# An idle row copied ahead of ScalarE's last chunk, and eight tokens' adds given to GpSimd

## The chip, the cores and the metric

One core of a Trainium2 chip runs the whole program. The metric is the time of one execution on the device in microseconds (us): lower is better. Three runs of the kernel before gave 105.50, 105.60 and 105.89 us, median 105.60 us.

## What is computed

The input `x` is (2, 2048, 512), and `cond` is (2, 512). A rate neuron turns each channel into spikes, and a two-layer network is applied to the spikes, with w1 (512, 2048) and w2 (2048, 512):

```python
rates = relu(x) * 0.001
c = cond[:, None, :] + cumsum(rates, axis=1)
fl = floor(c)
prev = concatenate([floor(cond)[:, None, :], fl[:, :-1, :]], axis=1)
spikes = (fl - prev) / 0.001
h = relu(spikes @ w1 + b1)
out = x + h @ w2 + b2
```

A channel's sum rises so slowly that it crosses a whole number about once in 2048 tokens. So nearly every token has no spike at all, and its output is `x` plus one fixed row, `relu(b1) @ w2 + b2`. This is called the idle row. The tokens with a spike are the exceptions.

## The kernel before

**Layout.** Each batch of 2048 tokens lies in SBUF as `x_sb[b]`, 128 partitions by 16 tokens by 512 channels, in float32. Four tokens of the 16 make a piece (`TQ = 4`), and a piece is the unit in which the result goes out: 1 MB, eight pieces in all. "Piece (b, q)" is tokens 4q to 4q+3 of batch b.

**Loading.** SyncE loads the x blocks and the sixteen row pairs of w1 transposed and w2. While they arrive, ScalarE makes from each chunk m of w1 the change that one spike of each channel makes in the hidden layer (`table_chunk`), TensorE multiplies it by w2 into the four PSUM banks `ps_table` (`table_part(m, begin, end)`: the column blocks begin to end of chunk m), and VectorE sums x by blocks of 16 tokens.

**The idle row.** VectorE sums five of the sixteen terms in `idle_part`. TensorE adds the others in strips of 32 partitions (`add_strips`) in `ps_idle`. ScalarE copies the strips to `idle_base`, TensorE joins them into the full row on all partitions (`join_strips`, again in `ps_idle`), and ScalarE copies that to SBUF as `idle_row`. VectorE can read the row from PSUM, and GpSimd reads the SBUF copy. Both have a function `add_idle(b, begin, end)`, which adds the row to the tokens begin to end of batch b. VectorE's is one instruction for the whole stretch, and GpSimd's is one instruction for each token.

**VectorE's chain.** For each batch, VectorE finds which token each channel spikes in (`find_tokens`), TensorE spreads these over all partitions (`spread_tokens`), VectorE compares them (`count_met`, four instructions `same`) and marks the first channel of each token (`find_leads`), TensorE counts (`count_leads`), VectorE makes a one-hot table (`find_slots`, outputs `slot` and `hot`), TensorE turns this into a list (`list_rows`), and VectorE writes row numbers (`list_rows`, output `row_at`). GpSimd then gathers rows of w1 by these numbers (`get_rows(b)`, two indirect DMAs to `spiking_rows`). After batch 1's list come `find_row_tokens`, TensorE's `spread_row_tokens` and VectorE's `turn_others`. From there on TensorE runs the two layers for the tokens in which several channels spike (`first_layer`, `second_layer`). Small operations for checks and lists follow on VectorE: `find_odd`, `count_crowd`, `list_singles`, `list_general`, `judge`.

**Output.** SyncE issues one 1 MB store per piece, in a fixed order, and waits before each for the piece's `idle_added`. Once all four stores of a batch have landed (`idle_stored[b]`), GpSimd issues four indirect DMAs (L368, `add_row`) that add table rows to the tokens with a single spike. Between the two batches' adds it gathers a row of x (L403). At the end it writes the several-spike tokens' rows (L414), which need TensorE's second layer and the `row_ready` that VectorE raises.

**What sets the order.** Each engine runs its own instructions in the order written, and the engines wait for each other on semaphores only. The semaphore `reading_psum` is raised by VectorE at the start of `count_met(1)` and again after `find_row_tokens`. GpSimd waits for it before its adds.

## Time and profile before

| | us |
|---|---|
| median of three runs | 105.60 |
| the profiled execution, whole | 105.66 |
| its span, first to last instruction | 103.9 |
| TensorE (PE) busy | 89.3 (86%) |
| VectorE (DVE) busy | 72.3 (70%) |
| GpSimd (POOL) busy | 45.5 (44%) |
| ScalarE (ACT) busy | 35.6 (34%) |

1.76 us of the execution lie outside the span. The mean granted TensorE clock is 0.95 of full speed. The program loads for the first 45 us or so, computes lists while the DMA engines are nearly idle, and from about 66 us on writes its output.

### The profile page before, as it was taken

What the parts mean: (1) busy time and instruction counts of PE and PEld (TensorE: products, weight loads), DVE (VectorE), ACT (ScalarE), POOL (GpSimd) and SP (SyncE); (2) the same over time, 40 slices, a digit from 0 to 9 for tenths busy, and PEclk for the clock granted to TensorE, in tenths of its full rate; (3) what the DMA queues carried; (4) which work ended last, traced back from release to release, by engine and by line L of the source; (5) the groups of instructions that cost most, each with busy time, mean ns of one, the idle gap of its engine ahead of it and who ended that gap; (6) DMA issues with size and microseconds to landing.
All of it is one profiled execution on the core that took longest, in us unless ns stands there. A gap on an engine that the chain in (4) does not pass through costs nothing.

```text
span 103.9 us, 1032 instructions
## 1 busy us (share of the span) xinstructions
PE 89.3 (86%) x299; PEld 44.9 (43%) x299; DVE 72.3 (70%) x164; ACT 35.6 (34%) x64; POOL 45.5 (44%) x46
## 2 busy tenths in 40 slices
PE   5999999998999999899999999992999999990000
PEld 5944444442644423552345444422997445420000
DVE  2439899999695969899896998699999912002200
ACT  2867525325255550579071000061677000000000
POOL 6598000000077600037303802899900478747860
PEclk9999999999999999999999999999589999999655
DMA  2999999999999999930000610599999999997881
GB/s 77 298 378 393 413 423 413 412 408 402 413 412 408 390 398 392 406 151 8 6 3 0 145 70 0 180 363 372 410 432 404 416 416 321 297 208 144 100 115 62
DMA packets 8491, 28.72 MB, mean 276 GB/s; under 512 B 2024, under 2 KB 2152, under 8 KB 7303
## 3 DMA queue, kind: packets, MB, share of 16 engines
q1 hardware_dynamic: 6192, 25.43, 62.8%
q0 software_dynamic: 2144, 3.17, 15.1%
q8 instruction: 4, 0.07, 0.3%
q14 instruction: 5, 0.04, 0.1%
q10 hardware_dynamic: 146, 0.01, 0.1%
HBM read 21.58 MB, written 10.75 MB: 311 GB/s over the span
## 4 chain that ended last, share of the span: by engine, by line
SPq 21%; PE 19%; DVE 17%; DMA 16%; POOL 11%; issue 10%; POOLq 3%; DVEq 0%
DMA x_sb<-in_x 16%; PE ps_table L868 13%; SPq L290 13%; POOL out L368 9%; SPq L285 7%; DVE x_sb L737 7%; DVE over_two L710 4%; DVE same L645 3%; POOLq L60 2%; PE ps_idle L884 2%; DVE total_two L592 1%; PE ps_turn L905 1%; POOL out L414 1%; POOL general_x L403 1%; PE ps_idle L894 1%
## 5 line engine op out<-in xcount | busy, mean ns | idle before, releaser
L868 PE MATMUL ps_table<-w_sb 128*128 128x512 f32 x128 | 57.8, 598 | 0.0
L868 PEld LDWEIGHTS ps_table<-w_sb 128*128 128x128 f32 x128 | 23.2, 190 | 27.4 <-issue 25.1
L363 POOL DMA_INDIRECT rates<-in_x_turned,sixteen_at x8 | 9.3, 1166 | 31.4 <-DVE sixteen_at L606 29.6
L592 DVE SCALAR_TENSOR_TENSOR total_two<-x_sb,total_two 128x1024 f32<-128x1024 f32 x14 | 17.1, 1224 | 2.4 <-DMA x_sb<-in_x 2.1
L457 ACT ACTIVATE w_sb<-w_sb,b_col 128x512 f32<-128x512 f32 (+2 forms) x19 | 12.2, 643 | 16.9 <-DMA w_sb<-in_w_pairs 16.9
L368 POOL DMA_INDIRECT out<-w_sb,to_single x8 | 12.4, 1555 | 10.4 <-issue 8.6
L737 DVE TENSOR_TENSOR x_sb<-x_sb,ps_idle 128x2048 f32<-128x2048 f32 (+2 forms) x8 | 13.8, 1750 | 0.7 <-DVE row_token L694 0.2
L974 PE MATMUL ps_met<-w_sb 128*128 128x512 f32 x32 | 14.2, 596 | 0.0
L458 ACT ACTIVATE w_sb<-w_sb,minus_relu_b 128x512 f32<-128x512 f32 (+2 forms) x19 | 12.3, 649 | 0.6
L375 POOL TENSOR_TENSOR x_sb<-x_sb,idle_row 128x512 f32<-128x512 f32 x8 | 9.9, 1265 | 0.1
L974 PEld LDWEIGHTS ps_met<-w_sb 128*128 128x128 f32 x32 | 5.9, 190 | 6.7 <-issue 6.5
L387 POOL DMA_INDIRECT spiking_rows<-in_w,row_at x4 | 4.0, 1006 | 10.6 <-DVE row_at L680 9.9
L493 ACT ACTIVATE w_sb<-ps_table 128x512 f32<-128x512 f32 x4 | 2.4, 597 | 13.3 <-PE ps_table L868 13.3
L788 DVE TENSOR_TENSOR general_x<-general_x,b_row 128x512 f32<-128x512 f32 x1 | 0.7, 693 | 8.0 <-DMA general_x<-in_x,from_general 8.0
L548 DVE SCALAR_TENSOR_TENSOR idle_part<-w_sb,relu_b,idle_part 128x512 f32<-128x512 f32 x5 | 3.8, 758 | 2.0 <-DMA w_sb<-in_w_pairs 1.9
L979 PE MATMUL ps_small<-ones 128*128 128x128 f32 x16 | 3.7, 429 | 1.1 <-POOLq L337 1.1
L979 PEld LDWEIGHTS ps_small<-ones 128*128 128x128 f32 x16 | 3.5, 331 | 1.1 <-POOLq L337 1.1
L955 PE MATMUL ps_turn<-ident,spiking_rows 128*128 128x128 f32 x6 | 2.0, 328 | 2.2 <-issue 2.2
L710 DVE TENSOR_TENSOR over_two<-block_sum,theta_sum 128x8 f32<-128x8 f32 x1 | 3.7, 3726 | 0.0
L354 POOL MEMSET spiking_rows<- 128x2048 f32 x2 | 3.5, 1798 | 0.0
L645 DVE SCALAR_TENSOR_TENSOR same<-ps_turn,token,weigh 128x512 bf16<-128x512 f32 x4 | 3.0, 751 | 0.7 <-PE ps_turn L917 0.6
L884 PE MATMUL ps_idle<-w_sb,relu_b 128*32 128x512 f32 x22 | 3.2, 604 | 0.0
(142 smaller groups left out, 84.8 us busy)
## 6 DMA issues: line engine op xcount, KB each, us to landing
x_sb<-in_x SPq DMA_DIRECT2D x16, 512.0 KB, 14.7
out<-x_sb SPq DMA_DIRECT2D x8, 1024.0 KB, 7.9
w_sb<-in_w_pairs SPq DMA_DIRECT2D x15, 512.0 KB, 16.0
w_sb<-in_w_pairs SPq DMA_DIRECT2D x2, 256.0 KB, 2.9
b_row<-in_b SPq DMA_DIRECT2D x1, 256.0 KB, 14.7
rates<-in_x_turned,sixteen_at POOLq DMA_INDIRECT x8, 6.2
out<-w_sb,to_single POOLq DMA_INDIRECT x8, 6.3
spiking_rows<-in_w,row_at POOLq DMA_INDIRECT x4, 4.2
```

The costliest lines, as they stand in the source:

```text
L285: sp.dma_start(w_sb[:, m, :, :], w_pairs[m * P:(m + 1) * P, :, :]).then_inc(w_in[m], 16)
L290: sp.dma_start(x_sb[b][:, tokens, :], x_blk[b, :, tokens, :]).then_inc(x_in[b][half], 16)
L363: pool.indirect_dma_start(out=rates[:, col, :], out_offset=None, in_=x_sixteen, in_offset=bass.IndirectOffsetOnAxis(ap=sixteen_at[:, col:c ...
L368: pool.indirect_dma_start(out=out_rows, out_offset=bass.IndirectOffsetOnAxis(ap=to, axis=0), in_=row, in_offset=None, bounds_check=last_ro ...
L375: last = pool.tensor_tensor(x_sb[b][:, t, :], x_sb[b][:, t, :], idle_row[:, :], ALU.add)
L457: chain(act.activation(weights, weights, ACT.Relu, bias=b1_col[:, m:m + 1], scale=PER_DT))
L458: act.activation(weights, weights, ACT.Identity, bias=minus_relu_b1[:, m:m + 1]).then_inc(table_hidden_ready, 1)
L592: chain(dve.scalar_tensor_tensor(out=total_two[b][:, :, :], in0=tokens, scalar=0.0, in1=total_two[b][:, :, :], op0=ALU.max, op1=ALU.add))
L710: dve.tensor_tensor(over_two[:, :].rearrange("p (b c) -> p b c", b=B), block_sum[:, :, :, P], theta_sum[:, 1, :].rearrange("p (b c) -> p b ...
L737: last = dve.tensor_tensor(tokens, tokens, along(ps_idle[:, :], end - begin), ALU.add)
L868: last = pe.matmul(ps_table[c][:, :], table_hidden[:, m, c * P:(c + 1) * P], w2_sb[:, m, :], start=(m == 0), stop=(m == FC - 1))
L974: last = pe.matmul(to[:, :], hidden[m], w2_sb[:, m, :], start=(m == 0), stop=(m == FC - 1))
```

## The change

Four things change.

1. In TensorE's order, all strips are added together, and the join follows one column block later, ahead of `count_leads(0)`.
2. ScalarE copies the joined row to `idle_row` ahead of chunk 15's two activations instead of behind them.
3. GpSimd adds the row to tokens 0 and 1 of batch 0 as soon as the copy is there, then issues `get_rows(0)`, adds to tokens 2 to 5, issues `get_rows(1)` and adds to tokens 6 and 7. None of these eight adds waits for `reading_psum`. Tokens 12 to 15 of batch 1 stay with GpSimd and wait for `reading_psum` 2. GpSimd has twelve adds instead of eight.
4. VectorE loses its adds for tokens 0 to 7 of batch 0 and gets tokens 12 to 15 of it. All its adds stand behind `turn_others`, and the small operations stand ahead of it. SyncE stores in the order (0,0), (0,1), (0,2), (0,3), (1,0), (1,1), (1,3), (1,2).

```diff
@@ SyncE
-            for b, q in ((0, 0), (0, 3), (0, 1), (0, 2), (1, 3), (1, 0), (1, 1), (1, 2)):
+            for b, q in ((0, 0), (0, 1), (0, 2), (0, 3), (1, 0), (1, 1), (1, 3), (1, 2)):
@@ GpSimd
+            pool.wait_ge(idle_copied, 1)
+            add_idle(0, 0, 2)
             get_rows(0)
-            pool.wait_ge(idle_copied, 1)
-            pool.wait_ge(reading_psum, 1)
-            add_idle(0, 12, 13)
+            add_idle(0, 2, 6)
             get_rows(1)
+            add_idle(0, 6, 8)
             pool.wait_ge(reading_psum, 2)
-            add_idle(0, 13, 16)
             add_idle(1, 12, 16)
@@ ScalarE
                 if m == FC - 2:
                     act.wait_ge(strips_summed, 1)
                     act.activation(idle_base[:, :], ps_idle[:, :], ACT.Copy).then_inc(strips_copied, 1)
-            act.wait_ge(idle_summed, 1)
-            act.activation(idle_row[:, :], ps_idle[:, :], ACT.Copy).then_inc(idle_copied, 1)
+                    act.wait_ge(idle_summed, 1)
+                    act.activation(idle_row[:, :], ps_idle[:, :], ACT.Copy).then_inc(idle_copied, 1)
@@ VectorE
             find_leads(1)
-            add_idle(0, 0, 1)
             find_slots(1)
-            add_idle(0, 1, 2)
             list_rows(1)
             find_row_tokens()
-            dve.sem_inc(reading_psum, 1)
-            add_idle(0, 2, 4)
-            turn_others()
-            add_idle(0, 4, 8)
-            add_idle(0, 8, 12)
             find_odd()
             count_crowd()
-            add_idle(1, 0, 4)
             list_singles()
             list_general()
+            turn_others()
+            dve.sem_inc(reading_psum, 1)
+            add_idle(0, 8, 12)
+            add_idle(0, 12, 16)
+            add_idle(1, 0, 4)
             add_idle(1, 4, 8)
             add_idle(1, 8, 12)
             judge()
@@ TensorE
-            add_strips(4, 8)
-            table_part(11, 0, 2)
+            add_strips(4, FC - BY_HAND + 1)
+            table_part(11, 0, 1)
+            join_strips()
             count_leads(0)
-            table_part(11, 2, 3)
-            add_strips(8, FC - BY_HAND + 1)
-            table_part(11, 3, DC)
-            join_strips()
+            table_part(11, 1, DC)
             list_rows(0)
```

GpSimd's instructions from the last gather of x (L363) to the first scatter-add (L368), before:

```order
L363 DMA rates<-in_x_turned,sixteen_at 128x16 [waits sixteen_listed]
L363 DMA rates<-in_x_turned,sixteen_at 128x16 x3
L387 DMA spiking_rows<-in_w,row_at 128x2048 [waits rows_listed,rows_cleared]
L387 DMA spiking_rows<-in_w,row_at 128x2048 [waits rows_listed]
L375 TENSOR_TENSOR x_sb<-x_sb,idle_row 128x512 [waits reading_psum,idle_copied]
L387 DMA spiking_rows<-in_w,row_at 128x2048 [waits rows_got0,rows_listed,rows_cleared]
L387 DMA spiking_rows<-in_w,row_at 128x2048 [waits rows_got1,rows_listed]
L375 TENSOR_TENSOR x_sb<-x_sb,idle_row 128x512 [waits reading_psum]
L375 TENSOR_TENSOR x_sb<-x_sb,idle_row 128x512 x6
L368 DMA out<-w_sb,to_single 4096x512 [waits table_rows_ready,idle_stored0,singles_listed]
```

The same place on GpSimd in the changed kernel:

```order
L375 TENSOR_TENSOR x_sb<-x_sb,idle_row 128x512 [waits idle_copied]
L375 TENSOR_TENSOR x_sb<-x_sb,idle_row 128x512
L387 DMA spiking_rows<-in_w,row_at 128x2048 [waits rows_listed,rows_cleared]
L387 DMA spiking_rows<-in_w,row_at 128x2048 [waits rows_listed]
L375 TENSOR_TENSOR x_sb<-x_sb,idle_row 128x512 x4
L387 DMA spiking_rows<-in_w,row_at 128x2048 [waits rows_got0,rows_listed,rows_cleared]
L387 DMA spiking_rows<-in_w,row_at 128x2048 [waits rows_got1,rows_listed]
L375 TENSOR_TENSOR x_sb<-x_sb,idle_row 128x512 x2
L375 TENSOR_TENSOR x_sb<-x_sb,idle_row 128x512 [waits reading_psum]
L375 TENSOR_TENSOR x_sb<-x_sb,idle_row 128x512 x3
```

Two adds now stand ahead of the first pair of gathers, and four ahead of the second pair, where there was one.

TensorE around the join of the strips (`ps_idle<-idle_base,strip_first`) and batch 0's count (`leads_run,upper`), before:

```order
L884 MATMUL ps_idle<-w_sb,relu_b 32x512 x4
L868 MATMUL ps_table<-w_sb 128x512 x2
L923 MATMUL ps_small<-leads_run,upper 128x2
L868 MATMUL ps_table<-w_sb 128x512
L884 MATMUL ps_idle<-w_sb,relu_b 32x512 x3
L888 MATMUL ps_idle<-idle_part,ones 32x512
L868 MATMUL ps_table<-w_sb 128x512
L894 MATMUL ps_idle<-idle_base,strip_first 128x512
L938 MATMUL ps_small<-named,hot 128x4 x4
```

The same place on TensorE in the changed kernel, whose lines are numbered three lower:

```order
L881 MATMUL ps_idle<-w_sb,relu_b 32x512 x7
L885 MATMUL ps_idle<-idle_part,ones 32x512
L865 MATMUL ps_table<-w_sb 128x512
L891 MATMUL ps_idle<-idle_base,strip_first 128x512
L920 MATMUL ps_small<-leads_run,upper 128x2
L865 MATMUL ps_table<-w_sb 128x512 x3
L935 MATMUL ps_small<-named,hot 128x4 x4
```

The join moved ahead of the count and of three of chunk 11's column blocks. What TensorE does up to `list_rows(0)` is the same in sum.

## Rows read from the trace of the kernel before

**Rows 1.** Timeline of GpSimd, last part: start, length, line, operation, [idle before <-releaser].

```profile
82.00 1.61 POOL L368 DMA_INDIRECT out<-w_sb,to_single  x1 [6.78 <-issue]
...
89.46 1.01 POOL L403 DMA_INDIRECT general_x<-in_x,from_general  x1 [0.30 <-issue]
92.24 1.56 POOL L368 DMA_INDIRECT out<-w_sb,to_single  x1 [1.77 <-DMA out<-x_sb]
...
99.66 1.03 POOL L414 DMA_INDIRECT out<-w_sb,to_general  x1 [0.31 <-issue]
```

**Rows 2.** Windows of the output phase; the last two columns are DMA share and GB/s.

```profile
core 0: us, PE busy (x) PEld busy (x) DVE busy (x) ACT busy (x) POOL busy (x), PEclk, DMA share, GB/s
...
70.30:75.20 4.90, 2.99 (x18) 3.02 (x19) 4.90 (x3) 1.97 (x6) 4.90 (x5) 0.77 0.97 400
75.20:82.00 6.80, 6.80 (x39) 5.37 (x39) 6.45 (x14) 3.98 (x12) 0.02 (x2) 0.91 1.01 413
82.00:92.20 10.20, 10.20 (x27) 4.64 (x26) 2.33 (x6) 0.00 (x0) 7.25 (x5) 1.00 1.03 334
```

**Rows 3.** Timeline of VectorE from 64 us: three of its idle-row adds and `find_odd`.

```profile
64.57 1.22 DVE L737 TENSOR_TENSOR x_sb<-x_sb,ps_idle 128x1024 f32<-128x1024 f32 x1 [0.24 <-DVE row_token L694]
...
71.52 3.73 DVE L710 TENSOR_TENSOR over_two<-block_sum,theta_sum 128x8 f32<-128x8 f32 x1
...
79.08 4.48 DVE L737 TENSOR_TENSOR x_sb<-x_sb,ps_idle 128x2048 f32<-128x2048 f32 x2
```

**Rows 4.** Timeline of GpSimd, 56 to 76 us: gathers and adds.

```profile
56.03 1.02 POOL L387 DMA_INDIRECT spiking_rows<-in_w,row_at  x1 [5.36 <-DVE row_at L680]
...
58.39 1.28 POOL L375 TENSOR_TENSOR x_sb<-x_sb,idle_row 128x512 f32<-128x512 f32 x1
64.25 1.00 POOL L387 DMA_INDIRECT spiking_rows<-in_w,row_at  x1 [4.58 <-DVE row_at L680]
...
66.59 8.63 POOL L375 TENSOR_TENSOR x_sb<-x_sb,idle_row 128x512 f32<-128x512 f32 x7
```

**Rows 5.** Timeline of ScalarE, 48 to 55 us.

```profile
48.74 0.72 ACT L458 ACTIVATE w_sb<-w_sb,minus_relu_b 128x512 f32<-128x512 f32 x1
52.51 0.60 ACT L482 ACTIVATE idle_base<-ps_idle 128x512 f32<-128x512 f32 x1 [3.05 <-PE ps_idle L888]
...
54.39 0.60 ACT L484 ACTIVATE idle_row<-ps_idle 128x512 f32<-128x512 f32 x1
```

**Rows 6.** Timeline of TensorE, 53 to 73 us (x counts records).

```profile
53.33 1.02 PE L894 MATMUL ps_idle<-idle_base,strip_first 128*128 128x512 f32 x2
...
60.28 0.38 PE L923 MATMUL ps_small<-leads_run,upper 128*128 128x2 f32 x2
...
62.68 0.25 PE L938 MATMUL ps_met<-named,hot 128*128 128x4 bf16 x4
...
66.42 3.60 PE L868 MATMUL ps_table<-w_sb 128*128 128x512 f32 x8
72.21 0.30 PE L955 MATMUL ps_turn<-ident,spiking_rows 128*128 128x128 f32 x1 [2.19 <-issue]
```

**Rows 7.** Timeline of VectorE, 51 to 60 us: five steps of its chain.

```profile
51.98 1.29 DVE L671 TENSOR_TENSOR hot<-slot,slot_name 128x512 bf16<-128x512 f32 x2
...
54.59 0.15 DVE L633 SCALAR_TENSOR_TENSOR token<-tokens_under,token_base 128x4 f32<-128x4 f32 x1
...
55.09 0.15 DVE L680 TENSOR_TENSOR row_at<-row_of,ps_small 128x1 int32<-128x1 f32 x1
...
56.11 0.75 DVE L645 SCALAR_TENSOR_TENSOR same<-ps_turn,token,weigh 128x512 bf16<-128x512 f32 x1 [0.61 <-PE ps_turn L917]
...
59.29 0.40 DVE L652 SCALAR_TENSOR_TENSOR is_first<-met,valid 128x4 f32<-128x4 f32 x1
```

**Rows 8.** Windows around `first_layer`; the third column from the right is the granted clock.

```profile
73.00:76.50 3.50, 3.50 (x19) 3.50 (x18) 3.25 (x6) 2.15 (x7) 2.22 (x2) 0.52 1.00 412
76.50:79.20 2.70, 2.70 (x26) 2.70 (x26) 2.60 (x8) 2.62 (x9) 0.00 (x0) 1.00 1.05 428
```

## The prediction

> **What bounds the kernel now.** I read the end first, on GpSimd's timeline. The last instruction (L414, at 99.66) stands behind four scatter-adds that start at 92.24, and these were released by a DMA: the last store of batch 1 [rows 1]. From that release on, everything is GpSimd's fixed queue of about 8.5 us plus the landing of the last write, so the end moves one to one with the landing of the eighth store. One step back, batch 0's scatter-adds start at 82.00 when batch 0's stores have landed, and with the gather at L403 they end at 90.47, which is 1.8 us ahead of the 92.24. They are next in line but not the bound [rows 1]. The next question is why the last store lands at 92 when VectorE's last add is done at 79.08 + 4.48 = 83.56 [rows 3]. The windows answer that: the DMA engines are busy 0.97, 1.01 and 1.03 of the time in every stretch from 70.3 to 92.2 [rows 2]. The output phase is a DMA queue that never runs dry. What counts is when it fills up, and how much is out of the way by then.
>
> The first store leaves at 64.57 + 1.22 = 65.8 [rows 3]. The second one, piece (0,3), waits for GpSimd's tokens 13 to 15, the first three of a run of seven adds in 8.63 us, so 1.233 us each: 66.59 + 3 x 1.233 = 70.3 [rows 4]. From 70.3 the other seven pieces and batch 0's scatter-adds take to 92.2, 21.9 us [rows 2]. I call 70.3 the **bulk start**, and my sum is about how far it moves.
>
> **The row comes earlier.** The second half of the strips ended just before ScalarE's copy at 52.51, after 3.05 us of waiting, with chunk 14 done at 48.74 + 0.72 = 49.46 [rows 5]. Now the strips end at about 49.5, and the join stands ahead of three column blocks and the count. A block costs 3.60/4 = 0.9 us [rows 6], so the join moves from 53.33 to about 50.5, and the copy `idle_row`, which ended at 54.39 + 0.60 = 55.0 [rows 5], ends at about 52.0. TensorE's work up to `list_rows(0)` is the same in sum, so this costs nothing there. Batch 0's count is about 1 us later but still ends as VectorE gets to `find_slots(0)`. Chunk 15 on ScalarE is 1.5 us of work that TensorE needs only at about 66 [rows 6]. Nothing.
>
> **Two adds ahead of the first gathers.** GpSimd starts tokens 0 and 1 at about 52.0, and 2 x 1.233 = 2.5 us is over before batch 0's gathers can start at 56.03 [rows 4]. On GpSimd alone this is free. But VectorE starts `hot` at 51.98 and runs straight on to `token`, 54.59 + 0.15 = 54.74 [rows 7]. What an add on GpSimd does to such an operation is to be seen twice before. `find_odd` is an operation of 8 elements a partition, with both inputs in SBUF. It starts at 71.52 and lasts 3.73 us, to 75.25 [rows 3], and GpSimd's run of seven ends at 66.59 + 8.63 = 75.22 [rows 4]. `is_first`, with two SBUF inputs too, takes 0.40 and ends at 59.69 [rows 7], and GpSimd's single add ends at 58.39 + 1.28 = 59.67 [rows 4]. VectorE's own adds, with one input in PSUM, and the `same` operations run beside GpSimd's adds at their full speed (2.24 us a piece, 0.75 us) [rows 3, 7]. So I read: a VectorE operation with two SBUF inputs does not run while GpSimd adds, and does not get in between two of GpSimd's adds either. The three adds from 71.52 to 75.22 kept `find_odd` out all the time.
>
> The Trainium skill says the same against this change, in "SBUF — State Buffer", section "Who interferes with whom": a VectorE instruction with two SBUF inputs and a GpSimd instruction that reads SBUF exclude each other, and whoever issues first keeps the port for the whole instruction. Read literally, VectorE would get in after one add at most. The trace agrees on the exclusion and goes further, with 3.73 us for three adds. By the literal rule `find_leads`, whose four operations form three dependent steps, would lose up to one add at each step instead of the whole run at its first, and the list below would come about 0.8 us earlier than I put it: 110.5 us instead of 111.3.
>
> `hot` and `find_tokens(1)` are nearly all of the two-input kind. They lose 2.5 us whichever of the two is first. `token` is ready at 57.2 instead of 54.74. TensorE was 0.7 us behind it and now waits for it. Counting from `token`, `same` started 1.37 us later, because TensorE was late [rows 7]. Now only the spread of 0.45 us and VectorE's own 0.75 us for `list_rows(0)` lie between. So `same` starts at 58.0, **+1.9**, and ends at 61.2. The row numbers (55.09) move by the full 2.5, and with them the gathers from 56.03 to 58.5 and the end of the pair from 58.39 to 60.85 [rows 4, 7].
>
> **Four adds ahead of the second gathers.** They run from 60.85 to 60.85 + 4 x 1.233 = 65.8. `is_first` wants to start at 61.2, inside that run, and gets through at 65.8 instead of 59.69: **+6.1**. This is the largest term. If `find_leads` (0.5 us) should slip in ahead of the adds, the next operations, `slot` and `hot`, are shut out to 65.8 instead. As find_leads and the count are then done, the delay is 1.4 us smaller. TensorE's count (60.28) moves to 66.4 and the last of `list_rows(1)` (62.68 + 0.25 = 62.93) to 69.0 [rows 6].
>
> **TensorE's clock.** Before, TensorE idled for 2.19 us ahead of 72.21 [rows 6], and from 73.0 to 76.5 the granted clock was 0.52, the level of 1.2 GHz [rows 8]. In the change it idles for about 4 us ahead of the count. Between the count and the list lie 2.5 us of its work (60.28 to 62.93). At the low level all of that would take twice as long, at the high one nothing is added: 0 to 2.5. I take **1.0**, as the low level before came some time after the idle began and lasted 3.5 us, so that part of it should be spent waiting. The list is then at 70.0.
>
> **The bulk start after.** The second pair of gathers moves with the list, less the 0.2 us by which an add of VectorE's was in its way (that add is gone): 64.25 + 6.1 + 1.0 - 0.2 = 71.15. The pair takes 2.3 us (64.25 to 66.59), and tokens 6 and 7 another 2.5. Piece (0,1) is ready at **75.9**. VectorE waits for `turn_others`, which needs TensorE's next four blocks (62.93 to about 66.6 before), so it starts its adds at about 74.1 and has (0,2) at 76.4, so that this is no faster. The small operations cost nothing: they fit in this wait, and there is no GpSimd add then. `find_odd` no longer loses 3.6 us. VectorE's five pieces take 5 x 2.24 = 11.2 us to 85.3, GpSimd's (1,3) is done at about 81, and the DMA queue, with 7 MB from 76, stays full.
>
> Piece (0,0) is ready with token 3 at 60.85 + 2.5 = 63.3. It is out before the bulk, as it was before, when it was done (with the gathered rows beside it) by about 70.
>
> **The sum.** Bulk start 75.9 against 70.3 is +5.6 us. The bulk itself is the same seven pieces and the same scatter-adds: 21.9 us, and the end's fixed queue behind it. GpSimd's batch 0 adds move along. The last row needs the second layer: TensorE's `first_layer` starts behind table chunk 15, at 66.42 + 3.60 + 7.1 = 77.1 instead of 72.21 [rows 6], which is less than the rest moves by and had 3 us to spare. 105.66 + 5.6 = **111.3 us** (the profiled execution is 0.06 above the median).
>
> **The rivals.**
> *VectorE keeps its place in the first round (107.9 us).* The trace of before has no case in which GpSimd comes while VectorE is in a chain of short operations with gaps of 0.04 us. If GpSimd has to wait until that chain stops at 54.74, its two adds end at 57.2, the gathers move by 1.5 only, and the four adds run from 59.8 to 64.8. `find_leads` is through by then, and `hot` is what waits: list at 66.7, +3.8. The bulk start is then at 72.6, +2.3. For it: the chain's gaps are short. Against it: `find_odd` shows how a waiting side fares, and GpSimd arrives at the very gap ahead of `hot`.
> *No real blocking (104.3 us, faster).* The lists come as before. The second gathers are at 64.0, tokens 6 and 7 are done at 69.0, (0,2) at 69.4, and (0,0) has left at 60.9. The bulk starts 1.3 us earlier, so 105.66 - 1.3. TensorE would also start `first_layer` up to 2 us earlier, which gains nothing at the end. This is what the change says it does. Against it stand the 3.73 and the 0.40. The sign turns where the list is delayed by 1.3 us: one add of 1.233 in the way is enough to eat the gain.
> *Worse than forecast (113 us).* The low clock covers all of the work between count and list, and half of the chunk behind it. Or the gathered rows land late and meet the bulk.
>
> **How the numbers follow.** Forecast, with its own range 109.5 to 112.7 (find_leads slipping in, clock 0 to 2.5): 0.58. VectorE first: 0.20. No blocking: 0.12. Worse: 0.06. Delays that happen to cancel the 1.3 us: 0.04. A measurement of this kernel can tell about 0.5% from no change. So faster 0.12, same 0.04, slower 0.84. The range leaves out the faster case, the same and half of the worse ones: 106.7 to 113.0.
>
> **What would show it.** In the changed kernel's trace: `hot` or an operation of `find_tokens(1)` of over 1 us that ends with GpSimd's second add; `is_first` of 4 us or more that ends with GpSimd's fourth; TensorE idle ahead of `spread_tokens(1)` and for 4 us ahead of `count_leads(1)`; the second gathers at 70 to 72; `find_odd` back at 0.2 us; the second store at 74 to 77; batch 1's scatter-adds at about 98. I am wrong if `is_first` takes under 1 us, or if the DMA queue takes less than 20 us for the seven pieces.

## Result and profile after

The changed kernel takes 112.12 us (median of 4 runs, 111.63 to 112.73) against 105.55 us for the kernel before in the same comparison. The ratio is 1.063, with a 95% interval of 1.056 to 1.070. The forecast was 111.3 us in a range of 106.7 to 113.0. The profiled execution took 111.98 us with a span of 110.2 us, so the span grew by 6.3 us.

GpSimd's timeline of the changed kernel (start, length, operation, [idle before <-releaser]), to set beside [rows 1] and [rows 4]:

```profile
51.86 2.94 POOL L375 TENSOR_TENSOR x_sb<-x_sb,idle_row 128x512 f32<-128x512 f32 x2 [1.26 <-ACT idle_row L484]
58.11 1.03 POOL L387 DMA_INDIRECT spiking_rows<-in_w,row_at  x1 [3.31 <-DVE row_at L680]
...
60.48 4.92 POOL L375 TENSOR_TENSOR x_sb<-x_sb,idle_row 128x512 f32<-128x512 f32 x4
71.89 1.01 POOL L387 DMA_INDIRECT spiking_rows<-in_w,row_at  x1 [6.49 <-issue]
...
74.22 2.50 POOL L375 TENSOR_TENSOR x_sb<-x_sb,idle_row 128x512 f32<-128x512 f32 x2
...
98.33 1.56 POOL L368 DMA_INDIRECT out<-w_sb,to_single  x1 [1.77 <-DMA out<-x_sb]
```

Read it from the bottom. Batch 1's scatter-adds start at 98.33 instead of 92.24, 6.1 us later, again released by the last store. The second pair of gathers starts at 71.89 instead of 64.25. Between the four adds, which end at 65.40, and these gathers GpSimd does nothing for 6.5 us: it waits for the row numbers.

VectorE's timeline of the changed kernel shows why, beside [rows 3] and [rows 7]:

```profile
51.89 3.46 DVE L671 TENSOR_TENSOR hot<-slot,slot_name 128x512 bf16<-128x512 f32 x2
...
56.66 0.16 DVE L633 SCALAR_TENSOR_TENSOR token<-tokens_under,token_base 128x4 f32<-128x4 f32 x1
...
57.76 0.75 DVE L645 SCALAR_TENSOR_TENSOR same<-ps_turn,token,weigh 128x512 bf16<-128x512 f32 x1 [0.19 <-PE ps_turn L914]
...
60.94 4.49 DVE L652 SCALAR_TENSOR_TENSOR is_first<-met,valid 128x4 f32<-128x4 f32 x1
...
73.52 3.24 DVE L707 TENSOR_TENSOR to_single<-token,not_single 128x8 int32<-128x8 f32 x1
...
77.58 11.08 DVE L737 TENSOR_TENSOR x_sb<-x_sb,ps_idle 128x2048 f32<-128x2048 f32 x5 [0.24 <-DVE others_turn L700]
```

The two `hot` operations take 3.46 us instead of 1.29. `is_first`, an operation on four elements a partition, takes 4.49 us and ends at 65.43, when GpSimd's fourth add ends (65.40). `to_single`, on eight elements, takes 3.24 us and ends at 76.76, when the adds to tokens 6 and 7 end (76.72).

TensorE's timeline of the changed kernel, beside [rows 6]:

```profile
53.77 0.24 PE L935 MATMUL ps_small<-named,hot 128*128 128x4 bf16 x4
55.41 0.25 PE L935 MATMUL ps_met<-named,hot 128*128 128x4 bf16 x4 [1.39 <-DVE hot L671]
...
66.02 0.59 PE L920 MATMUL ps_small<-leads_run,upper 128*128 128x2 f32 x2 [4.14 <-DVEq L660]
66.47 0.56 PE L922 MATMUL ps_small<-leads_run,ones 128*128 128x2 f32 x2
66.89 3.76 PE L865 MATMUL ps_table<-w_sb 128*128 128x512 f32 x4
...
70.60 0.25 PE L935 MATMUL ps_met<-named,hot 128*128 128x4 bf16 x4
```

It idles for 4.14 us ahead of `count_leads(1)`, and then runs the two table blocks in 3.76 us where they took half as long before. The windows of the changed kernel give the clock (the last three columns are the granted clock, the DMA share and GB/s):

```profile
60.00:65.00 5.00, 1.88 (x5) 0.57 (x3) 4.93 (x5) 0.00 (x0) 4.97 (x5) 1.00 0.62 207
65.00:66.00 1.00, 0.00 (x0) 0.00 (x0) 0.84 (x4) 0.00 (x0) 0.40 (x1) 0.60 0.98 393
66.00:71.00 5.00, 4.98 (x17) 2.73 (x18) 1.85 (x6) 0.00 (x0) 0.00 (x0) 0.50 0.06 26
71.00:72.00 1.00, 1.00 (x2) 0.48 (x2) 0.87 (x8) 0.00 (x0) 0.11 (x1) 0.50 0.00 0
```

All the work between the count and the list ran at the level of 1.2 GHz.

### The profile page after: what moved, and what is told of

It is laid out like the page before. It is cut to its first block, busy times and chain, and to the rows that moved or that the text cites. A ratio compares the mean times of both kernels' runs of the same rounds, so it can differ in the third digit from the quotient of the medians.

```text
span 110.2 us, 1031 instructions
## 1 busy us (share of the span) xinstructions
PE 91.2 (83%) x299; PEld 45.4 (41%) x299; DVE 75.9 (69%) x161; ACT 35.2 (32%) x64; POOL 50.4 (46%) x50
## 4 chain that ended last, share of the span: by engine, by line
DVE 28%; SPq 20%; DMA 15%; POOL 14%; issue 12%; PE 5%; POOLq 2%; DVEq 0%
DMA x_sb<-in_x 15%; SPq L290 13%; POOL out L368 10%; SPq L285 6%; DVE same L645 6%; DVE is_first L652 4%; POOL x_sb L375 3%; PE ps_table L865 3%; DVE hot L671 3%; DVE to_single L707 3%; POOLq L60 1%; POOLq L278 1%; DVE x_sb L737 1%; DVE total_two L592 1%; POOL general_x L403 1%
## 5 line engine op out<-in xcount | busy, mean ns | idle before, releaser
L865 PE MATMUL ps_table<-w_sb 128*128 128x512 f32 x128 | 61.1, 627 | 0.0
L865 PEld LDWEIGHTS ps_table<-w_sb 128*128 128x128 f32 x128 | 24.8, 202 | 28.5 <-issue 27.4
L363 POOL DMA_INDIRECT rates<-in_x_turned,sixteen_at x8 | 8.8, 1101 | 31.9 <-DVE sixteen_at L606 30.0
L368 POOL DMA_INDIRECT out<-w_sb,to_single x8 | 12.4, 1554 | 9.1 <-issue 7.4
L375 POOL TENSOR_TENSOR x_sb<-x_sb,idle_row 128x512 f32<-128x512 f32 x12 | 15.3, 1306 | 2.2 <-ACT idle_row L484 1.3
L737 DVE TENSOR_TENSOR x_sb<-x_sb,ps_idle 128x2048 f32<-128x2048 f32 x5 | 11.1, 2281 | 0.2 <-DVE others_turn L700 0.2
L493 ACT ACTIVATE w_sb<-ps_table 128x512 f32<-128x512 f32 x4 | 2.4, 598 | 23.7 <-PE ps_table L865 23.7
L671 DVE TENSOR_TENSOR hot<-slot,slot_name 128x512 bf16<-128x512 f32 x4 | 4.8, 1228 | 0.1
L652 DVE SCALAR_TENSOR_TENSOR is_first<-met,valid 128x4 f32<-128x4 f32 x2 | 4.6, 2324 | 0.1
L920 PE MATMUL ps_small<-leads_run,upper 128*128 128x2 f32 x4 | 0.9, 286 | 4.1 <-DVEq L660 4.1
L707 DVE TENSOR_TENSOR to_single<-token,not_single 128x8 int32<-128x8 f32 x1 | 3.2, 3236 | 0.0
```

The source lines that it names most:

```text
L363: pool.indirect_dma_start(out=rates[:, col, :], out_offset=None, in_=x_sixteen, in_offset=bass.IndirectOffsetOnAxis(ap=sixteen_at[:, col:c ...
L368: pool.indirect_dma_start(out=out_rows, out_offset=bass.IndirectOffsetOnAxis(ap=to, axis=0), in_=row, in_offset=None, bounds_check=last_ro ...
L375: last = pool.tensor_tensor(x_sb[b][:, t, :], x_sb[b][:, t, :], idle_row[:, :], ALU.add)
L652: chain(dve.scalar_tensor_tensor(out=is_first[:, mine], in0=met[:, mine], scalar=NOT_FIRST - 0.5, in1=valid[:, mine], op0=ALU.is_lt, op1=A ...
L671: dve.tensor_tensor(hot[:, b, g, :, :], over(slot[:, b, g, :], P), along(slot_name[:, :], DC), ALU.is_equal).then_inc(hot_ready, 1)
L737: last = dve.tensor_tensor(tokens, tokens, along(ps_idle[:, :], end - begin), ALU.add)
```

## Experiments

The theory is that GpSimd's early adds shut VectorE's chain out, that the lists are late for that reason, and that the end follows the time at which the store queue fills. Its rivals are that the new order on TensorE costs the time, or that GpSimd's being busy ahead of the gathers does, or that the clock or the late small operations do.

### The TensorE and ScalarE part alone

```diff
 # on the kernel before
-            add_strips(4, 8)
-            table_part(11, 0, 2)
+            add_strips(4, FC - BY_HAND + 1)
+            table_part(11, 0, 1)
+            join_strips()
             count_leads(0)
-            table_part(11, 2, 3)
-            add_strips(8, FC - BY_HAND + 1)
-            table_part(11, 3, DC)
-            join_strips()
+            table_part(11, 1, DC)
 # and ScalarE's copy to idle_row ahead of chunk 15
```

> The kernel before with the TensorE and ScalarE part of the change alone: strips together, join ahead of the count, idle_row copied ahead of chunk 15. GpSimd, VectorE and SyncE as before. Theory (GpSimd's adds shut VectorE out): 105.6 us, no change, as no add of GpSimd moves (it still waits for reading_psum), with is_first at 0.2 to 0.4 us. Rival (the new order on TensorE delays batch 0's count or the lists): several us more, and idle time on TensorE ahead of count_leads(1).

It took 106.64 us (12 runs) against 105.79 (23 runs), a ratio of 1.007 with an interval of 1.004 to 1.010. So it is not free: this half of the change costs 0.7%. Its trace shows the way, one line each of ScalarE, TensorE and VectorE:

```profile
50.15 0.60 ACT L482 ACTIVATE idle_base<-ps_idle 128x512 f32<-128x512 f32 x1 [0.75 <-PE ps_idle L888]
```

```profile
50.80 1.12 PE L894 MATMUL ps_idle<-idle_base,strip_first 128*128 128x512 f32 x2 [0.51 <-issue]
```

```profile
52.17 0.37 DVE L665 SCALAR_TENSOR_TENSOR slot<-leads_run,ps_small,leads 128x4 f32<-128x4 f32 x2 [0.69 <-PE ps_small L923]
```

ScalarE starts the strips' copy only at 50.15. With a single block between the strips and the join, TensorE waits 0.5 us for it, the count behind the join is late, and VectorE waits 0.69 us in `find_slots(0)`. In the profiled run of the changed kernel ScalarE's copy happened to start at 49.29 and there was no such wait. Why it starts late here is not shown: the strips end at 49.24 and ScalarE's activation before it at 49.40, against 49.22 and 49.37 in the changed kernel. Of the eight profiled kernels in this text that have this order, four show the wait (this one, and those of the memsets, of the adds one by one and of the lists behind adds), and the others do not. The rival was right about the direction, but it accounts for about 0.7 of 6.6 us.

### Memsets in place of the early adds

```diff
 # on the changed kernel, GpSimd; scratch is 128 x 2800
             pool.wait_ge(idle_copied, 1)
-            add_idle(0, 0, 2)
+            chain(pool.memset(scratch[:, :], 0.0))
             get_rows(0)
-            add_idle(0, 2, 6)
+            chain(pool.memset(scratch[:, :], 0.0))
+            pool.sem_inc(idle_added[0][0], 1)
+            pool.memset(scratch[:, :], 0.0)
             get_rows(1)
```

> The changed kernel, but in place of GpSimd's six adds to tokens 0 to 5 of batch 0 it runs memsets of a scratch tile of 2800 elements a partition (by the memset row of before, 1.8 us for 2048, about 2.5 us each, as long as two adds). GpSimd is busy as long and as early, but reads no SBUF. Those six tokens stay without the row. Theory (VectorE's operations with two SBUF inputs are kept out by an operation of GpSimd that reads SBUF): hot and is_first take 0.7 and 0.2 us, the second pair of gathers starts at about 64, and the time is 104 to 105 us, below before. Rival (it is GpSimd's being busy, its queue ahead of the gathers, or the earlier store that costs the time): 111 to 113 us as in the changed kernel.

It took 105.39 us against 105.79, a ratio of 0.997 with an interval of 0.994 to 1.000. GpSimd is as busy and as early as in the changed kernel:

```profile
52.35 2.43 POOL L393 MEMSET scratch<- 128x2800 f32 x1 [2.08 <-ACT idle_row L487]
...
59.84 2.44 POOL L395 MEMSET scratch<- 128x2800 f32 x1
62.44 2.43 POOL L397 MEMSET scratch<- 128x2800 f32 x1 [0.15 <-POOL scratch L395]
```

VectorE in the same run:

```profile
52.30 1.29 DVE L674 TENSOR_TENSOR hot<-slot,slot_name 128x512 bf16<-128x512 f32 x2
53.51 1.32 DVE L629 TENSOR_SCALAR rates<-rates 128x64 f32<-128x64 f32 x1
...
60.31 0.16 DVE L655 SCALAR_TENSOR_TENSOR is_first<-met,valid 128x4 f32<-128x4 f32 x1
```

`hot` takes its 1.29 us under the first memset, and `is_first` its 0.16 under the second. The lists are in time again (the second gathers start at 65.0), and the 6.6 us are gone. GpSimd's being busy ahead of the gathers costs nothing here. What costs is that the adds read SBUF, which the memsets don't. This is the experiment that settles the cause.

One operation did wait: the `TENSOR_SCALAR`, with one SBUF input and an SBUF output, takes 1.32 instead of 0.19 us and ends at 54.83, with the memset (54.78). The Trainium skill has both halves in "SBUF — State Buffer", section "Who interferes with whom": a VectorE operation with two SBUF inputs contends with a GpSimd instruction that reads SBUF and not with one that only writes it, and a `tensor_scalar` can enter a two-port mode, in which it contends with GpSimd. The trace agrees with the first (0.16 us for `is_first`). The 1.32 us would fit the second, but no view shows the mode of an instruction.

### One add at a time

```diff
 # on the changed kernel, GpSimd's add_idle
-                    last = pool.tensor_tensor(x_sb[b][:, t, :], x_sb[b][:, t, :], idle_row[:, :], ALU.add)
+                    chain(pool.tensor_tensor(x_sb[b][:, t, :], x_sb[b][:, t, :], idle_row[:, :], ALU.add))
```

> The changed kernel, with each of GpSimd's adds waiting by a semaphore for the end of the one ahead. Theory (a run of adds is handed over at once, and a VectorE operation that comes later waits for all that were handed over; one at a time lets it in at the next boundary): is_first takes at most 1.3 us instead of 4.5, the steps of find_leads behind it wait for up to one add each, count_leads(1) starts 1 to 3 us earlier than in the changed kernel, to_single takes under 1.4 us, and the time is 109 to 111 us. Rival (VectorE gets in only when GpSimd has no add left to do): is_first 4.5 us or more, and 112 us or slightly more for the semaphores.

It took 109.52 us, a ratio of 1.037 (1.031 to 1.043) against 1.063 for the changed kernel: 2.6 us less, with the same adds in the same places and only waits added. VectorE in this run:

```profile
61.31 0.86 DVE L652 SCALAR_TENSOR_TENSOR is_first<-met,valid 128x4 f32<-128x4 f32 x1
...
65.13 2.30 DVE L671 TENSOR_TENSOR hot<-slot,slot_name 128x512 bf16<-128x512 f32 x2
...
70.30 1.89 DVE L707 TENSOR_TENSOR to_single<-token,not_single 128x8 int32<-128x8 f32 x1
```

`is_first` waits for the rest of one add (0.86 us instead of 4.49). The steps behind it wait for the next ones, so that `count_leads(1)` starts at 63.83, 2.2 us earlier than in the changed kernel. TensorE idles for 1.59 us instead of 4.14, and the clock stays at 1.00. `to_single` exceeded its bound of 1.4 us. It starts at 70.30, before GpSimd's next add begins at 70.87, and waits for that add too.

So the length of the wait follows the number of adds that come one behind the other without a wait, and not the number that have begun. That such a run is handed over to GpSimd at once is a reading of these lengths; no view shows the handing over. The memsets stood behind waits of their own too, but this is not why they were harmless: `is_first` ran for its 0.16 us in the middle of one, and here it waits out the rest of the add that it meets.

### Each round by itself

The two variants are x4 (the second round of adds only) and x3 (the first round only).

```diff
 # on the changed kernel, GpSimd: second round only
-            pool.wait_ge(idle_copied, 1)
-            add_idle(0, 0, 2)
             get_rows(0)
-            add_idle(0, 2, 6)
+            pool.wait_ge(idle_copied, 1)
+            add_idle(0, 0, 4)
             get_rows(1)
-            add_idle(0, 6, 8)
+            add_idle(0, 4, 8)
```

> The changed kernel without its two adds ahead of the first gathers: get_rows(0), four adds, get_rows(1), four adds. One look, for the marks and not for the time. Theory (each block of adds shuts VectorE out by itself): hot and find_tokens(1) run undisturbed, token is ready at about 55.3 (54.7 and 0.6 for the later count), is_first starts at about 59.8 and lasts until GpSimd's fourth add ends at 63.9, about 4 us, and TensorE idles 3 to 4 us ahead of count_leads(1). Rival (the first block is what makes the second collide): is_first under 1.3 us and lists as before.

```diff
 # on the changed kernel, GpSimd: first round only
             add_idle(0, 0, 2)
             get_rows(0)
-            add_idle(0, 2, 6)
             get_rows(1)
-            add_idle(0, 6, 8)
+            add_idle(0, 2, 8)
```

> The changed kernel without its four adds between the two pairs of gathers: two adds, get_rows(0), get_rows(1), six adds. One look, for the marks and not for the time, as piece (0,0) is late here and SyncE stores it first. Theory: hot and find_tokens(1) lose 2.0 to 2.5 us to the two adds, the first pair of gathers starts at 58 to 59, is_first takes 0.16 as GpSimd does no add then, list_rows(1) ends 1.5 to 2.5 us later than before (at 64.5 to 65.5), and TensorE idles 1 to 1.6 us ahead of spread_tokens(1) but hardly ahead of count_leads(1). With x4 the two blocks' delays add up to the changed kernel's. Rival (the first block is hidden behind TensorE's lag): list_rows(1) ends at 63 to 63.5.

With the second round only, `token` is ready at 54.68, as before. `is_first` on VectorE and the four adds on GpSimd end within 0.03 us of each other:

```profile
58.89 4.37 DVE L651 SCALAR_TENSOR_TENSOR is_first<-met,valid 128x4 f32<-128x4 f32 x1
```

```profile
58.31 4.92 POOL L375 TENSOR_TENSOR x_sb<-x_sb,idle_row 128x512 f32<-128x512 f32 x4
```

It ends at 63.26, 3.6 us later than the 59.69 of [rows 7]. TensorE idles for 4.03 us, and the list ends at 68.7 instead of 62.93. With the first round only, `hot` takes 2.37 us, `token` is ready at 56.62 and `is_first` takes 0.16. The list ends at 65.75, 2.8 us late instead of 1.5 to 2.5. The expectation missed a drop of the clock. TensorE waits 0.46 us ahead of batch 0's second list and 1.38 us ahead of the spread, and the windows from 57.2 to 58.0 and from 58.0 to 63.0 show 0.53 and 0.73. Waits of 0.19 and 1.38 us in the same places left it at 1.00 with one add at a time, so the lengths of the waits alone don't tell whether it falls. A single run each gave 112.34 us (second round) and 111.79 us (first round). Neither round alone is harmless, and in both variants the small operations hold up the stores as well. The delays of the list are 5.8 and 2.8 us, 8.6 in sum against 7.9 in the changed kernel, so they add up only roughly, and the times don't: either round alone costs nearly all of the 6.6 us. In the first-round variant GpSimd adds tokens 2 to 7 in one run behind the second gathers, so that piece (0,1) is ready at 76.5 although its list is 5.1 us earlier than in the changed kernel.

The first-round variant shows the longest wait of all. First VectorE, then GpSimd:

```profile
68.39 8.08 DVE L706 TENSOR_TENSOR to_single<-token,not_single 128x8 int32<-128x8 f32 x1
```

```profile
68.07 0.99 POOL L387 DMA_INDIRECT spiking_rows<-in_w,row_at  x1 [0.30 <-issue]
69.08 7.37 POOL L375 TENSOR_TENSOR x_sb<-x_sb,idle_row 128x512 f32<-128x512 f32 x6
```

An operation of eight elements waits from 68.39 to 76.47 for six adds, of which the first begins 0.69 us after it. The gather alone holds nothing: in the kernel before, an operation with two SBUF inputs (L614, `under`) runs its usual 0.69 us from 49.79 on, inside a gather that lasts from 49.72 to 50.67. It is the adds queued behind the gather that go first. The Trainium skill gives GpSimd an instruction queue of eight entries ("TensorE: Matmul & The Clock Gate", in the note on engine queue depths). That would fit, but no run here shows the queue itself.

### TensorE kept busy in the wait

```diff
 # on the changed kernel, TensorE
             table_part(13, 0, 2)
+            pe.wait_ge(rows_listed, GROUPS)
+            for _ in range(18):
+                pe.matmul(ps_small[:, 2 * P:3 * P], ones[:, :], ones[:, :], start=True, stop=True)
             count_leads(1)
```

> The changed kernel with 18 matmuls of 128 columns on constants ahead of count_leads(1), 0.22 us each at the full clock, about 4 us in all, in the place where TensorE idled for 4.1 us. They write columns of a PSUM bank that nothing reads. Theory (the idle time costs a clock drop on the way to list_rows(1), 2.1 us there, which comes on top of the wait for VectorE): the granted clock stays at 1.00 from 60 to 72 us, count_leads(1) starts at 66.0 to 66.5 as in the changed kernel, list_rows(1) ends at about 69 instead of 70.8, and the time is 110.0 to 110.8 us. Rival (the lists' delay is VectorE's alone and the clock does not matter for the end): list_rows(1) moves, but the time stays within 0.5% of 112.1.

It took 110.38 us, a ratio of 1.040 (1.033 to 1.047), against 1.063 (1.056 to 1.070) for the changed kernel: 1.7 us less, and 2.4 us by the ratios, as the kernel before took 106.13 us in this group. It is what the theory said, and the rival's "within 0.5%" is excluded. TensorE in this run:

```profile
61.39 4.18 PE L1004 MATMUL ps_small<-ones 128*128 128x128 f32 x36
65.71 0.38 PE L920 MATMUL ps_small<-leads_run,upper 128*128 128x2 f32 x2
...
68.10 0.25 PE L935 MATMUL ps_met<-named,hot 128*128 128x4 bf16 x4
```

`count_leads(1)` starts at 65.71, close to the 66.02 of the changed kernel, because it waits for VectorE. The granted clock is 1.00 from 60 to 92 us, and the list ends at 68.35. From the count's start to the list's end it takes 2.6 us instead of 4.8. So about 2 of the 6.6 us are the clock's (1.7 by the times, 2.4 by the ratios), and they come on top of VectorE's wait.

### The lists behind VectorE's adds

```diff
 # on the changed kernel, VectorE
             find_odd()
             count_crowd()
-            list_singles()
-            list_general()
             turn_others()
             dve.sem_inc(reading_psum, 1)
             add_idle(0, 8, 12)
             add_idle(0, 12, 16)
             add_idle(1, 0, 4)
+            list_singles()
+            list_general()
```

> The changed kernel with list_singles and list_general moved from ahead of turn_others to behind VectorE's third piece. Theory (the 3.24 us of to_single, which waits for GpSimd's adds to tokens 6 and 7, hold up VectorE's adds): others_turn starts at about 75.2 instead of 77.0, piece (0,2) is ready 1.8 us earlier, the dip of the DMA share at 80 to 81 us is gone, and the time is 0.6 to 1.5 us less, 110.6 to 111.5. Rival (the DMA queue is full anyway): no change, 112.1.

`others_turn` starts at 75.82 instead of 76.99, and the dip of the DMA share at 80 us, seen in the changed kernel's windows, is gone. First the changed kernel, then this one:

```profile
80.00:81.00 1.00, 1.00 (x11) 1.00 (x10) 1.00 (x1) 0.89 (x3) 1.00 (x2) 1.00 0.42 164
```

```profile
80.00:81.00 1.00, 1.00 (x11) 0.91 (x10) 1.00 (x2) 0.91 (x4) 1.00 (x1) 1.00 1.00 410
```

But it took 112.54 us, a ratio of 1.055 (1.048 to 1.062), which can't be told from the changed kernel's 1.063 (1.056 to 1.070). These intervals leave room for the gain of 0.6 us too. The traces speak for the rival: piece (0,2) is ready 1.2 us behind (0,1) here and 3.1 us behind it in the changed kernel, and from (0,1) to batch 1's scatter-adds both take 21.6 us. The wait of `to_single` delays piece (0,2), but the end follows the first of the seven pieces, and that is GpSimd's (0,1).

### The bulk start across the kernels

The prediction's sum stood on one number, the time from the first of the last seven pieces to batch 1's scatter-adds. The bulk start is the end of the add that completes the piece. The traces give it for every kernel:

| kernel | bulk start | scatter-adds of batch 1 | between |
|---|---|---|---|
| before | 70.3 | 92.24 | 21.9 |
| TensorE and ScalarE part alone | 70.9 | 92.64 | 21.8 |
| memsets for adds | 69.8 | 91.23 | 21.4 |
| one add at a time | 73.5 | 95.18 | 21.7 |
| TensorE kept busy | 74.2 | 96.25 | 22.1 |
| changed kernel | 76.7 | 98.33 | 21.6 |
| lists behind adds | 77.4 | 99.05 | 21.6 |
| second round only | 77.0 | 98.65 | 21.7 |
| first round only | 76.5 | 98.11 | 21.7 |
| x7, a candidate of the next section | 68.5 | 92.21 | 23.8 |
| x10, the other candidate | 67.7 | 91.83 | 24.1 |
| x10, a second time | 67.9 | 91.66 | 23.7 |

In the first nine rows the gap stays within 21.4 to 22.1 us while the bulk start moves over 7.6 us. In the last three it does not: the first of the seven pieces is ready 1.8 to 2.6 us earlier than before, and the end comes only 0.0 to 0.6 us earlier. The likely reason is that the piece comes while more of piece (0,0) and of the gathered rows is still in the queue, so that its start is no longer the moment at which the queue fills. In x7 the DMA share is 1.00 or close to it from 68 us on:

```profile
68.00:69.00 1.00, 1.00 (x3) 0.39 (x3) 1.00 (x2) 0.74 (x2) 1.00 (x1) 1.00 1.00 418
69.00:70.00 1.00, 1.00 (x3) 0.19 (x1) 1.00 (x1) 0.65 (x2) 1.00 (x2) 1.00 1.01 426
```

That reason was not tried by itself. The prediction used the 21.9 us for a bulk that starts later than before, with piece (0,0) out ahead of it, and there it holds. In these two candidates an earlier bulk start gained far less than one to one.

### More of VectorE's adds in its gaps

The candidate starts from the kernel before. It gives VectorE's idle-row adds, which read the row from PSUM and ran beside GpSimd's adds at full speed in every trace, more of the chain's gaps:

```diff
 # on the kernel before; x7 is this part alone, with the stores (0,0), (0,1), (0,3), (0,2), (1,3), ...
             list_rows(0)
+            add_idle(0, 0, 1)
             count_met(1)
             find_leads(1)
-            add_idle(0, 0, 1)
-            find_slots(1)
             add_idle(0, 1, 2)
+            find_slots(1)
+            add_idle(0, 2, 3)
             list_rows(1)
             find_row_tokens()
             dve.sem_inc(reading_psum, 1)
-            add_idle(0, 2, 4)
+            add_idle(0, 3, 4)
+            add_idle(0, 4, 6)
             turn_others()
-            add_idle(0, 4, 8)
+            add_idle(0, 6, 8)
             add_idle(0, 8, 12)
 # x10 has this as well: VectorE
-            find_odd()
-            count_crowd()
             add_idle(1, 0, 4)
-            list_singles()
-            list_general()
             add_idle(1, 4, 8)
+            find_odd()
+            count_crowd()
+            list_singles()
+            list_general()
             add_idle(1, 8, 12)
 # x10, GpSimd, and the stores (0,0), (0,1), (0,2), (0,3), (1,0), (1,1), (1,3), (1,2)
-            pool.wait_ge(reading_psum, 1)
-            add_idle(0, 12, 13)
             get_rows(1)
             pool.wait_ge(reading_psum, 2)
-            add_idle(0, 13, 16)
+            add_idle(0, 12, 16)
```

> A candidate on the kernel before. VectorE, which waits 0.6 us for TensorE's spread ahead of count_met(1), does its first add there, and two more while it waits for turn_others, so that piece (0,0) is ready 0.6 us earlier and piece (0,1) 1.2 us. SyncE stores (0,1) ahead of (0,3). No add of GpSimd moves. Theory (the end follows the time at which the DMA queue fills, and VectorE's adds, which read the row from PSUM, cost nothing in gaps): first store at 65.2, the time 0.5 to 1.0 us less than before, 104.6 to 105.2. Rival (the add in the gap runs into the spread and delays count_met(1) by as much, or the queue's later part decides): 105.6, no change.

> The candidate x7 with three more changes: GpSimd's single add beside count_met(1), which shut is_first out for 0.2 to 0.4 us, goes behind the second gathers; VectorE's find_odd, which waited 3.65 us for GpSimd's run of adds, goes with the other small operations behind its piece (1,1); SyncE stores in the order (0,0), (0,1), (0,2), (0,3), (1,0), (1,1), (1,3), (1,2). Theory: is_first takes 0.16, the first store leaves at 64.8 to 65.0, find_odd takes 0.2, the time is 0.8 to 1.4 us less than before, 104.2 to 104.8. Rival (the DMA queue is full from 67 us on in either, so only the first store's time counts): as x7.

> The candidate with the adds off VectorE's chain once more, in a group of its own, as the first measurement was just clear of no change (0.995, interval 0.9917 to 0.9983). Theory: a ratio of 0.990 to 0.998 again. Rival (the first was chance): an interval around 1.000.

x7 took 105.82 us against 106.13, a ratio of 0.997 (0.993 to 1.000). x10 took 105.53 us in the same comparison, 0.995 (0.992 to 0.998), and 105.52 against 105.86 in a second one, 0.997 (0.994 to 1.000). One of the two intervals excludes no change and the other touches it. The gain is 0.3 to 0.5%, less than the 0.8% at which x10's expectation began, and it is not settled that there is one. The two candidates can't be told apart, as x10's rival had it. The chain did most of what was expected:

```profile
58.94 0.16 DVE L650 SCALAR_TENSOR_TENSOR is_first<-met,valid 128x4 f32<-128x4 f32 x1
...
74.25 1.68 DVE L708 TENSOR_TENSOR over_two<-block_sum,theta_sum 128x8 f32<-128x8 f32 x1
```

`is_first` is at its 0.16, and the first store leaves at 64.7 instead of 65.8. `find_odd` still waits, for 1.68 us instead of 0.2, because GpSimd's run of eight adds lasts until 75.90. TensorE idles from about 69.4 to 74.3 here, longer than the 2.2 us before, and the slowest gather lands 9.2 us after its issue instead of 6.6. The gathered rows seem to share the queue with stores that come earlier now. That part is argued and was not tried by itself.

The second run of x10 shows one thing more, which the changed kernel alone would hide. TensorE idles for 3.49 us in it, and the clock stays at 1.00 behind that:

```profile
73.11 0.30 PE L955 MATMUL ps_turn<-ident,spiking_rows 128*128 128x128 f32 x1 [3.49 <-issue]
```

```profile
73.00:78.00 5.00, 4.89 (x44) 4.92 (x45) 4.46 (x13) 4.33 (x13) 3.13 (x3) 1.00 1.01 423
```

## Why the prediction was right

**The bound.** The end moves with the eighth store, and that with the bulk start. This held to within 0.7 us in nine kernels, and not in the two candidates, whose bulk starts earlier. The forecast 21.9 us between them was 21.6.

**The row earlier.** Right in the profiled run: `idle_row` is ready at 51.18 + 0.60 = 51.8, forecast 52.0. Wrong in its price. The step said "this costs nothing there" and "Nothing". The TensorE and ScalarE part alone costs 0.7%. In half of the profiles with this order the join stalls on ScalarE's copy, which is the likely reason. I had put the end of the strips beside ScalarE's last activation to within 0.1 us and left no room for a late copy.

**Two adds ahead of the first gathers.** `token` at 57.2 was 56.8, `same` at 58.0 was 57.8, the gathers at 58.5 were 58.1. One reading in it was wrong: "does not get in between two of GpSimd's adds either". In the first round VectorE's first `hot` did. It starts at 51.89 and waits for the first add only. TensorE uses it at 53.77, while GpSimd's second add, which lasts until 54.80, takes 1.71 us instead of 1.25:

```profile
53.09 1.71 POOL L375 TENSOR_TENSOR x_sb<-x_sb,idle_row 128x512 f32<-128x512 f32 x1
```

The second `hot` waited for the end of the pair, so `hot` and what follows came 2.1 and not 2.5 us later. This `hot` came 0.03 us behind the start of the first add. In three more traces (TensorE kept busy, the first round only, the lists behind the adds) a `hot` also got in between the two adds, when the first had just begun or had been held up by the `hot` before. In all the later steps, where VectorE's operation came 0.46 us or more into a run of adds or ahead of one that stood behind a gather, it waited for the whole run, as the reading says.

**Four adds ahead of the second gathers.** The largest term. `is_first` was to get through at 65.8, 6.1 us later. It got through at 65.43, 5.7 us later than 59.69. The memsets and the adds one by one show that this wait is the cause. The sum of 110.5 us, by which VectorE would get in after one add at most, is excluded by the 4.49 us. With a wait ahead of each add it did get in like that (0.86 us).

**The clock.** Mis-sized: 1.0 us, measured 2.2 us between the count's start and the list's end (4.83 against 2.65), near the upper bound of 2.5. The reason given, that part of the low level would be spent waiting and that it would last 3.5 us, was the mistake. The clock fell at about 65.2, only 0.8 us ahead of the count, and stayed low to 72.0, 6.8 us and not the 3.5 us of [rows 8]. With this the list ended at 70.85 instead of 70.0, the second gathers started at 71.89 instead of 71.15, and piece (0,1) was ready at 76.7 instead of 75.9.

**The small operations.** Wrong: "they fit in this wait, and there is no GpSimd add then". `to_single` lost 3.1 us to the adds of tokens 6 and 7, and VectorE's adds started at 77.58 instead of 74.1. So the queue did not stay full either: its share was 0.42 from 80 to 81 us. By the trace with the lists behind the adds this did no harm at the end, since (0,1) was first in any case.

**The sum.** +5.6 forecast, +6.3 measured in the profiled span, and +6.6 between the medians. The bulk start moved by 6.4 us, 0.8 more than forecast: the clock term was 1.2 us too small and the exclusion 0.4 us too large. So two errors partly cancelled. That the join did not stall in the profiled run is luck; it did in four of eight profiles with this order.

**The rivals.** VectorE got in for one operation only, so 107.9 us did not come. "No blocking", forecast at 104.3 us, was brought about by the memsets and measured 105.4. The median run is not the profiled one, which took 104.53 us, the shortest of the ten. In that one the bulk starts at 69.8 instead of the 69.0 of the forecast. The late join (0.74 us in `find_slots(0)`) and the `TENSOR_SCALAR` behind the memset (1.1 us) are in its way. What the longer runs of this kernel do otherwise is not shown.

## What to carry to other kernels

GpSimd's adds, which read SBUF, were not beside VectorE's work but in its way, wherever VectorE had two SBUF inputs, and a run of them without waits in between was paid as a whole by an operation of a few elements. So put such GpSimd work under VectorE's PSUM operations, or try to leave it to VectorE in its own waits with an operand in PSUM, which gained 0.5% at most here. Read a stall twice: once as waiting, and once as the work behind it on TensorE, which may then run at half the clock. And where a sum rests on the moment at which a queue fills, look at what is still in the queue at the new moment.

## What the runs showed of the hardware

- An operation of VectorE with two SBUF inputs waited for a whole run of GpSimd's adds, even for those that had not begun: 8.08 us for six adds, the first of which begins 0.69 us later. With a semaphore wait ahead of each add it waited for one (0.86 us). The exceptions are four traces in which a `hot` came at the start of a pair and waited for the first add only. What decides between the two is not shown.
- GpSimd waits too: the second add of that pair took 1.71 us instead of 1.25, as VectorE had got in between, and its first add took 1.67 us in the first-round variant, where VectorE's `hot` was 0.15 us ahead of it.
- GpSimd's memset held up one `TENSOR_SCALAR` from SBUF to SBUF (1.32 us instead of 0.19) and no operation with two SBUF inputs. Nor did a gather hold up one with two (0.69 us).
- After 4.14 us of idle time TensorE's clock was low for 6.8 us, from 65.2 to 72.0. After 2.19 us in the kernel before, it was low for about 3.4 us, from 72.9 to 76.3. But 2.42 us in x7 and 3.49 us in x10's second run left it at 1.00. Eighteen small matmuls in the idle time kept it at 1.00, and the kernel was 1.7 us faster with this additional work.
